# A two-layer graph kernel: VectorE's adjacency group is put directly behind x1, ahead of the statistics of x1

## The chip, the cores and the metric

One core of one Trainium2 chip runs the whole kernel. The metric is the device time of one launch in microseconds (us); the median of three runs of the kernel before is 2405.9 us.

## The reference

128 graphs of 128 nodes with 512 features, each with its own 128x128 weighted adjacency. Cut to what is computed:

```python
h = relu(layernorm(x));  A_hat = adj + I;  d = A_hat.sum(-1) ** -0.5
x1 = x + (A_hat * d[:, None] * d[None, :]) @ (h @ W + b)            # layer 0
xh = relu(layernorm(x1))                                           # layer 1
H = (adj != 0);  Be = 1 / H.sum(columns);  Dn = 1 / (H @ adj[0])
P = H @ diag(Be) @ H.T
h1 = layer_norm(relu(Dn * (P @ (xh @ W1.T)) + b1)) * gamma + beta   # 1024 wide
out = Dn * (P @ (h1 @ W2.T)) + b2 + xh + x1
```

## The kernel before

Every engine has its own instruction stream, written out by hand; semaphores tie them together, and each engine works strictly in its own order. One step of the software pipeline works on four graphs at once: `p = k+1` is prepared (statistics of x, adjacency, h0), `a = k` goes through layer 0, `c1 = k-1` through the first product of layer 1, `c2 = k-2` through the second, and `o = k-3` is written out. Steps -1 to 4 and the last ones are unrolled, those between run in a hardware loop, two steps to an iteration. There are 128 graphs, so 127 steps have both `a` and `p`.

Products are done in two parts, a high and a low one (names with `_hi`, `_lo`, `h`, `l`), three matmuls for each. What a step of TensorE does, in order: row sums and t0 (L times h0, 2 + 12 small matmuls, waits for `L_lo` and `h0_lo`); t1 (P times xh, 12 small ones, waits for `xh_lo`); t2 (P times hn, 24 small ones, waits for `hn_lo`); y1 (24 wide ones, line 331); y0 (12 wide ones); the transpose of the next graph's scaled adjacency (line 399, into `ps_at`, here AT); y2 (24 wide ones), with the incidence product P (lines 315, 316) after the first eight.

VectorE's order from the end of y0 to t2 is: `x1` (line 664, reads y0 out of PSUM), `bn_stats` of x1 (667), `inv_r` (671), `bn_aggr` (672), `hn` (677), `dn1` (682), `h0_lo` (689), `P_lo` (694), then the adjacency group: `ahat_T` (701, AT plus a diagonal), `H_T` with its count (703), `inv_b` (707), `L_hi` (712), `inv_t` (714), `L_lo` (716); behind it `xh_lo` (722) and `hn_lo` (728). All these write small or [128, 512] and [128, 1024] tiles in SBUF.

GpSimd in the same stretch first turns the statistics of h into `sc2` (lines 794 to 803), then waits for the statistics of x1 and turns them into `sc1` (807 to 813). Behind these come `sum2 = scr2 + b2` (818) and `base2 = sum2 + vq` (822), each 128x512, and then nothing until `base0` (762) of the next step. ScalarE makes `hn_hi` from sc2, `P_hi`, and from sc1 `xh` (518) and then `xh_hi` (522); `xh_lo` on VectorE needs both of these.

Of the kernel before, what the change touches and what calls it, by code (L numbers as in the profile page):

```python
# [5 lines left out]
def bass_adjacency_prenorm_two_layer_gnn_kernel(  # L6
# [38 lines left out]
    ALU = mybir.AluOpType  # L45
# [10 lines left out]
    P_SCALE = 2.0 ** 8  # L56
# [14 lines left out]
    with ctx:  # L71
        def sb(name, shape, dt=F32):
            return ctx.enter_context(nc.sbuf_tensor(name, shape, dt))

        def sem(name):
            return ctx.enter_context(nc.semaphore(name))
# [27 lines left out]
        diag_d = sb("diag_d", [128, N])  # L104
        adj_d = sb("adj_d", [128, N])
        ahat_T = sb("ahat_T", [128, N])
        L_hi, L_lo = sb("L_hi", [128, N], F16), sb("L_lo", [128, N], F16)
        H_T = sb("H_T", [128, 2, N], F16)
# [24 lines left out]
        rd0 = sb("rd0", [128, 2, 2])  # L133
# [5 lines left out]
        deg, cnt = sb("deg", [128, 2]), sb("cnt", [128, 2])  # L139
        inv_b, inv_t = sb("inv_b", [128, 1]), sb("inv_t", [128, 1])  # L140
# [17 lines left out]
        AT = ps_at[:, 0:N]  # L158
# [18 lines left out]
        s_diag, s_adjd, s_at, s_ht = sem("diag_D_ready"), sem("D_adj_ready"), sem("adjT_in_psum"), sem("HT_parts_ready")  # L177
        s_ahat, s_lth, s_lt = sem("ahatT_ready"), sem("LT_hi_ready"), sem("LT_lo_ready")
        s_stat0, s_ln0 = sem("stats0_ready"), sem("ln0_scalars_ready")
        s_h0, s_h0h, s_h0l = sem("h0_ready"), sem("h0_hi_ready"), sem("h0_lo_ready")  # L180
        s_t0, s_t0h, s_t0l = sem("t0_in_psum"), sem("t0_hi_ready"), sem("t0_lo_ready")
# [5 lines left out]
        s_p, s_ph, s_pl = sem("P_in_psum"), sem("P_hi_ready"), sem("P_lo_ready")  # L187
# [12 lines left out]
        s_cnt, s_cntsafe, s_cntinv, s_hbhi = sem("cnt_ready"), sem("cnt_safe"), sem("cnt_inverted"), sem("HB_hi_ready")  # L200
# [7 lines left out]
        def live(g, i):  # L208

            return not isinstance(i, int) or 0 <= g < NG  # L210
# [7 lines left out]
        def wait(eng, s, i, g):  # L218

            if not isinstance(i, int) or g >= 0:  # L220
                eng.wait_ge(s, i + (g + 1))
# [311 lines left out]
        def _(dve):  # L533
# [33 lines left out]
            def step(i, k):  # L567
                p, a, c1, c2, o = k + 1, k, k - 1, k - 2, k - 3
                if live(o, i):

                    m = o % 2
# [6 lines left out]
                                             in1=base2[:, m, :], op0=ALU.mult, op1=ALU.add).then_inc(s_out, 1)  # L578
                if live(c1, i):
# [4 lines left out]
                    m = c1 % 2  # L584
# [7 lines left out]
                                             in1=q[:, m:m + 1], op0=ALU.mult, op1=ALU.mult).then_inc(s_qdn, 1)  # L592
                if live(a, i):
# [8 lines left out]
                    m = a % 2  # L602
# [5 lines left out]
                                             in1=HB_hi[:, m, :], op0=ALU.mult, op1=ALU.subtract)\  # L608
# [8 lines left out]
                if live(p, i):  # L617

                    m = p % 2
# [4 lines left out]
                                             op0=ALU.not_equal, op1=ALU.mult, accum_out=deg[:, m:m + 1])\  # L624
# [9 lines left out]
                if live(c1, i):  # L634

                    m = c1 % 2
                    for c in range(NCH):
# [4 lines left out]
                                                 in1=b1_all[:, cols], op0=ALU.mult, op1=ALU.add)\  # L642
# [6 lines left out]
                if live(a, i):  # L649

                    m = a % 2
# [5 lines left out]
                if live(a, i):  # L657

                    m = a % 2
                    wait(dve, s_y0, i, a)  # L660
                    wait(dve, s_base0, i, a)
                    wait(dve, s_base2, i, a - 2)
                    wait(dve, s_xh, i, a - 2)
                    dve.scalar_tensor_tensor(out=x1[:, m, :], in0=ps_y0[:, :], scalar=1.0 / (L_SCALE * X_SCALE),  # L664
                                             in1=base0[:, :], op0=ALU.mult, op1=ALU.add).then_inc(s_x1, 1)
                    wait(dve, s_x1, i, a)
                    dve.bn_stats(raw1[:, :], x1[:, m, :]).then_inc(s_raw1, 1)  # L667
                    wait(dve, s_raw1, i, a)
                    wait(dve, s_ln1, i, a - 1)
                    wait(dve, s_degsafe, i, a)  # L670
                    dve.reciprocal(inv_r[:, :], inv_d[:, :]).then_inc(s_deginv, 1)
                    dve.bn_aggr(st1[:, :], raw1[:, :]).then_inc(s_stat1, 1)
# [6 lines left out]
                if live(a, i):  # L679
                    m = a % 2  # L680
                    wait(dve, s_deginv, i, a)
                    dve.scalar_tensor_tensor(out=dn1[:, m:m + 1], in0=deg[:, m:m + 1], scalar=0.0,
                                             in1=inv_r[:, :], op0=ALU.is_gt, op1=ALU.mult).then_inc(s_dn1, 1)
# [6 lines left out]
                if live(a, i):  # L690
                    m = a % 2
                    wait(dve, s_ph, i, a)
                    wait(dve, s_t2, i, a - 2)
                    dve.tensor_tensor(P_lo[:, m, :], PP, P_hi[:, m, :], ALU.subtract).then_inc(s_pl, 1)  # L694
                if live(p, i):

                    m = p % 2
                    wait(dve, s_at, i, p)
                    wait(dve, s_diag, i, p)
                    wait(dve, s_lt, i, p - 1)  # L700
                    dve.tensor_tensor(ahat_T[:, :], AT, diag_d[:, :], ALU.add).then_inc(s_ahat, 1)  # L701
                    wait(dve, s_p, i, p - 2)
                    dve.tensor_scalar(H_T[:, m, :], AT, 0.0, None, ALU.not_equal, ALU.add,  # L703
                                      accum_out=cnt[:, m:m + 1]).then_inc(s_cnt, 1)
                    wait(dve, s_cnt, i, p)

                    dve.tensor_scalar(inv_b[:, :], cnt[:, m:m + 1], 1.0, 1.0 / P_SCALE, ALU.max, ALU.mult)\
                       .then_inc(s_cntsafe, 1)
                    wait(dve, s_ahat, i, p)
                    wait(dve, s_ln0, i, p)  # L710
                    wait(dve, s_t0, i, p - 1)
                    dve.tensor_scalar(L_hi[:, :], ahat_T[:, :], rd0[:, m, 1:2], None, ALU.mult).then_inc(s_lth, 1)  # L712
                    wait(dve, s_cntsafe, i, p)
                    dve.reciprocal(inv_t[:, :], inv_b[:, :]).then_inc(s_cntinv, 1)
                    wait(dve, s_lth, i, p)
                    dve.scalar_tensor_tensor(out=L_lo[:, :], in0=ahat_T[:, :], scalar=rd0[:, m, 1:2],  # L716
                                             in1=L_hi[:, :], op0=ALU.mult, op1=ALU.subtract).then_inc(s_lt, 1)
                if live(a, i):
                    m = a % 2
                    wait(dve, s_xhh, i, a)  # L720
# [2 lines left out]
                                             op0=ALU.mult, op1=ALU.subtract).then_inc(s_xhl, 1)  # L723
# [7 lines left out]
                if first_graph(i, c1):  # L731
                    scale_v()
                    split_w2(range(KH - 2))

            every_step(ENG.DVE, step)


# [121 lines left out]
```

## Time and profile before

| what | value |
|---|---|
| runs, median (lowest, highest) | 2405.9 us (2403.88, 2405.99) |
| span of the profiled execution | 2403.2 us |
| time of that execution around its span | not given apart; the median of the runs lies 2.7 us above the span |
| TensorE matmul busy | 2211.9 us, 92% |
| VectorE busy | 2115.8 us, 88% |
| GpSimd busy | 1334.4 us, 56% |
| ScalarE busy | 1158.7 us, 48% |
| mean granted TensorE clock | 0.995 |
| one step inside the loop | 18.40 and 18.34 us in turn |

Busy is the time in which an engine had an instruction under way. An engine that waits inside an instruction, for a port for example, is counted as busy. Line numbers are those of the kernel before.

### The profile page before, as it was taken

Reading aid. Unit: us, or ns where it says so; the run is one execution under the profiler, and the core shown is the slowest. Engines: PE = TensorE matmul, PEld = TensorE weight load, DVE = VectorE, ACT = ScalarE, POOL = GpSimd, SP = SyncE. Lnnn points to the kernel's source line nnn. Section 1 sums busy time; section 2 is a strip of 40 time slices with the busy share of each in tenths; the row PEclk is TensorE's granted clock in tenths of the full one; section 3 lists DMA queues with packets and bytes.
Section 4 is the critical chain, followed back from the end, with each engine's and each line's share of the span. In section 5 each row is a group of like instructions: output and inputs, shape, how many; then the busy total and the mean of one; then the engine's idle time right before and its main releaser. Section 6 shows DMA issues by size and latency. Waiting matters only on the chain.

```text
span 2403.2 us, 48798 instructions
## 1 busy us (share of the span) xinstructions
PE 2211.9 (92%) x14480; PEld 1799.3 (75%) x14480; DVE 2115.8 (88%) x4754; ACT 1158.7 (48%) x1809; POOL 1334.4 (56%) x2574
## 2 busy tenths in 40 slices
PE   6999999999999999999999999999999999999998
PEld 4777777777777777777777777777777777777776
DVE  6889888988898898889888988988898889888986
ACT  4444445454444444444444444444444454544443
POOL 3555555555555555555555555555555555555553
PEclk8999999999999999999999999999999999999999
DMA  3111111011111111111111111111111111111110
GB/s 134 34 37 33 38 39 33 33 39 37 33 33 39 37 33 36 40 33 33 39 38 33 33 39 37 33 33 40 36 33 38 38 33 33 39 37 33 33 37 19
DMA packets 76558, 90.39 MB, mean 38 GB/s; under 512 B 8576, under 2 KB 41344, under 8 KB 76544
## 3 DMA queue, kind: packets, MB, share of 16 engines
q1 hardware_dynamic: 76544, 90.22, 12.5%
q8 instruction: 7, 0.11, 0.0%
q14 instruction: 7, 0.06, 0.0%
HBM read 56.63 MB, written 33.55 MB: 38 GB/s over the span
## 4 chain that ended last, share of the span: by engine, by line
PE 56%; DVE 33%; issue 8%; DVEq 1%; ACT 0%; DMA 0%; POOL 0%; SPq 0%; POOLq 0%; ACTq 0%
PE ps_y L331 29%; PE ps_t L331 15%; DVE L_hi L712 7%; PE ps_t L306 5%; DVE L_lo L716 4%; DVE raw L667 4%; DVE x L664 4%; PE ps_t L308 4%; PE ps_t L307 4%; DVE hn_lo L728 3%; DVE h_lo L689 2%; DVE xh_lo L722 2%; DVE P_lo L694 1%; DVE H_T L703 1%; DVE ahat_T L701 1%
## 5 line engine op out<-in xcount | busy, mean ns | idle before, releaser
L762 POOL TENSOR_TENSOR base<-scr,x_t 128x512 f32<-128x512 f32 x128 | 165.7, 1294 | 706.6 <-ACT scr L474 706.6
L450 ACT ACTIVATE h<-z 128x512 f32<-128x512 f32 x256 | 161.8, 632 | 453.6 <-DVE z L641 453.6
L565 DVE BATCH_NORM_STATS2 raw<-h 128x6 f32<-128x512 f32 x256 | 177.8, 695 | 189.2 <-ACT h L450 189.2
L331 PE MATMUL ps_y<-w1h,t1h 128*128 128x512 f32 x1024 | 288.7, 404 | 0.7 <-ACT t1h L459 0.7
L331 PE MATMUL ps_y<-w1h,t1l 128*128 128x512 f32 x1024 | 275.2, 391 | 2.1 <-DVE t1l L582 2.1
L331 PE MATMUL ps_y<-w1l,t1h 128*128 128x512 f32 x1024 | 276.5, 392 | 0.0
L331 PE MATMUL ps_t<-w2h,t2h 128*128 128x512 f32 x1024 | 268.8, 405 | 1.1 <-ACT t2h L467 1.1
L331 PE MATMUL ps_t<-w2l,t2h 128*128 128x512 f32 x1024 | 266.7, 402 | 0.0
L459 ACT ACTIVATE t1h<-ps_t 128x512 fp32r<-128x512 f32 x128 | 76.4, 597 | 379.0 <-PE ps_t L308 379.0
L331 PE MATMUL ps_t<-w2h,t2l 128*128 128x512 f32 x1024 | 253.4, 390 | 0.0
L505 ACT ACTIVATE hn_hi<-h,sc 128x1024 f16<-128x1024 f32 x128 | 159.0, 1242 | 143.5 <-POOL sc L803 143.5
L331 PEld LDWEIGHTS ps_y<-w1l,t1h 128*128 128x128 f32 x1024 | 193.4, 189 | 42.8
L331 PEld LDWEIGHTS ps_y<-w1h,t1l 128*128 128x128 f32 x1024 | 192.9, 188 | 43.4 <-DVE t1l L582 2.5
L331 PEld LDWEIGHTS ps_t<-w2h,t2l 128*128 128x128 f32 x1024 | 192.3, 188 | 41.2
L331 PEld LDWEIGHTS ps_t<-w2h,t2h 128*128 128x128 f32 x1024 | 183.8, 189 | 45.9 <-ACT t2h L467 1.4
L306 PE MATMUL ps_t<-P_hi,hn_hi 128*128 128x128 f16 x1024 | 180.0, 220 | 34.9 <-issue 17.6
L331 PEld LDWEIGHTS ps_y<-w1h,t1h 128*128 128x128 f32 x1024 | 184.1, 190 | 32.1 <-ACT t1h L459 1.0
L331 PEld LDWEIGHTS ps_t<-w2l,t2h 128*128 128x128 f32 x1024 | 183.4, 189 | 32.5
L641 DVE SCALAR_TENSOR_TENSOR z<-ps_y,dn,b_all 128x512 f32<-128x512 f32 x256 | 185.2, 723 | 2.1 <-PE ps_y L331 2.1
L308 PE MATMUL ps_t<-P_hi,hn_lo 128*128 128x128 f16 x1024 | 179.7, 220 | 0.0
L307 PE MATMUL ps_t<-P_lo,hn_hi 128*128 128x128 f16 x1024 | 179.7, 220 | 0.0
L716 DVE SCALAR_TENSOR_TENSOR L_lo<-ahat_T,rd,L_hi 128x128 f16<-128x128 f32 x128 | 178.0, 1390 | 0.0
(117 smaller groups left out, 5998.8 us busy)
## 6 DMA issues: line engine op xcount, KB each, us to landing
x_t<-in_x_dram SPq DMA_DIRECT2D x128, 256.0 KB, 2.6
out_dram<-out_t SPq DMA_DIRECT2D x128, 256.0 KB, 2.0
adj_t<-in_adj_dram SPq DMA_DIRECT2D x128, 64.0 KB, 2.0
wrow_t<-in_adj_dram SPq DMA_DIRECT2D x128, 64.0 KB, 3.0
stage<-in_W1T_dram SPq DMA_DIRECT2D x1, 2048.0 KB, 11.6
stage<-in_W2T_dram SPq DMA_DIRECT2D x1, 2048.0 KB, 8.8
stage<-in_W_dram SPq DMA_DIRECT2D x1, 1024.0 KB, 8.5
b_all<-in_b_dram SPq DMA_DIRECT2D x2, 256.0 KB, 8.1
```

Of the source, the lines that this page charges most:

```text
L306: pe.matmul(ps, lh, rh, start=True, stop=False)
L307: pe.matmul(ps, lh, rl, start=False, stop=False)
L308: return pe.matmul(ps, ll, rh, start=False, stop=True)
L331: mm = pe.matmul(ps, t[:, j * 128:(j + 1) * 128], w[:, j, cols], start=(n == 0 and j == 0), stop=(n == 2 and j == blocks - 1))
L450: act.activation(h[:, cols], z[:, cols], ACT.Relu).then_inc(s_h[c], 1)
L505: act.activation(hn_hi[:, :], h[:, :], ACT.Identity, bias=sc2[:, 1:2], scale=sc2[:, 0:1]).then_inc(s_hnh, 1)
L565: dve.bn_stats(raw2[:, c, :], h[:, c * CH:(c + 1) * CH]).then_inc(s_raw2, 1)
L641: dve.scalar_tensor_tensor(out=z[:, cols], in0=ps_y1[:, cols], scalar=dn1[:, m:m + 1], in1=b1_all[:, cols], op0=ALU.mult, op1=ALU.add)\
L664: dve.scalar_tensor_tensor(out=x1[:, m, :], in0=ps_y0[:, :], scalar=1.0 / (L_SCALE * X_SCALE), in1=base0[:, :], op0=ALU.mult, op1=ALU.add) ...
L712: dve.tensor_scalar(L_hi[:, :], ahat_T[:, :], rd0[:, m, 1:2], None, ALU.mult).then_inc(s_lth, 1)
L716: dve.scalar_tensor_tensor(out=L_lo[:, :], in0=ahat_T[:, :], scalar=rd0[:, m, 1:2], in1=L_hi[:, :], op0=ALU.mult, op1=ALU.subtract).then_i ...
L762: pool.tensor_tensor(base0[:, :], scr0[:, :], x_t[:, m, :], ALU.add).then_inc(s_base0, 1)
```

## The change

VectorE's adjacency group for graph p moves from behind `P_lo` to directly behind `x1`. The statistics of x1, `hn`, `dn1`, `h0_lo` and `P_lo` follow behind it in their old order. No instruction and no wait is added or taken away; in the steps without `p` the order is as before. The other engines' streams are the same.

```diff
                     dve.scalar_tensor_tensor(out=x1[:, m, :], in0=ps_y0[:, :], ...).then_inc(s_x1, 1)
-                    wait(dve, s_x1, i, a)
-                    dve.bn_stats(raw1[:, :], x1[:, m, :]).then_inc(s_raw1, 1)
...
-                    dve.tensor_tensor(P_lo[:, m, :], PP, P_hi[:, m, :], ALU.subtract).then_inc(s_pl, 1)
                 if live(p, i):
                     m = p % 2
                     wait(dve, s_at, i, p)
                     wait(dve, s_diag, i, p)
                     wait(dve, s_lt, i, p - 1)
                     dve.tensor_tensor(ahat_T[:, :], AT, diag_d[:, :], ALU.add).then_inc(s_ahat, 1)
...
                                              in1=L_hi[:, :], op0=ALU.mult, op1=ALU.subtract).then_inc(s_lt, 1)
+                if live(a, i):
+                    m = a % 2
+                    wait(dve, s_x1, i, a)
+                    dve.bn_stats(raw1[:, :], x1[:, m, :]).then_inc(s_raw1, 1)
+                    wait(dve, s_raw1, i, a)
+                    wait(dve, s_ln1, i, a - 1)
+                    wait(dve, s_degsafe, i, a)
+                    dve.reciprocal(inv_r[:, :], inv_d[:, :]).then_inc(s_deginv, 1)
+                    dve.bn_aggr(st1[:, :], raw1[:, :]).then_inc(s_stat1, 1)
...
+                    dve.tensor_tensor(P_lo[:, m, :], PP, P_hi[:, m, :], ALU.subtract).then_inc(s_pl, 1)
                 if live(a, i):
                     m = a % 2
                     wait(dve, s_xhh, i, a)
```

## Rows read from the trace of the kernel before

**Rows 1.** The page's first lines: span, busy time of each engine.

```profile
span 2403.2 us, 48798 instructions
PE 2211.9 (92%) x14480; PEld 1799.3 (75%) x14480; DVE 2115.8 (88%) x4754; ACT 1158.7 (48%) x1809; POOL 1334.4 (56%) x2574
```

**Rows 2.** Waits, whole span: who waited <- releaser: us, times, longest.

```profile
PE ps_at L353 <- DVE L_lo L716: 134.2, 127, 3.7
...
PE ps_t L306 <- DVE hn_lo L728: 17.3, 61, 0.3
```

**Rows 3.** Timeline, VectorE, an even step: start us, us, engine, line, operation.

```profile
1207.82 0.69 DVE L664 SCALAR_TENSOR_TENSOR x<-ps_t,base 128x512 f32<-128x512 f32 x1 [0.21 <-PE ps_t L331]
1208.54 0.69 DVE L667 BATCH_NORM_STATS2 raw<-x 128x6 f32<-128x512 f32 x1
...
1209.43 0.78 DVE L677 TENSOR_SCALAR hn<-h,sc 128x1024 f32<-128x1024 f32 x1
...
1210.20 0.68 DVE L689 TENSOR_TENSOR h_lo<-h,h_hi 128x512 f16<-128x512 f32 x1
1210.80 0.28 DVE L694 TENSOR_TENSOR P_lo<-ps_p,P_hi 128x128 f16<-128x128 f32 x1
...
1211.63 1.40 DVE L712 TENSOR_SCALAR L_hi<-ahat_T,rd 128x128 f16<-128x128 f32 x1
...
1213.06 1.38 DVE L716 SCALAR_TENSOR_TENSOR L_lo<-ahat_T,rd,L_hi 128x128 f16<-128x128 f32 x1
1214.37 0.68 DVE L722 SCALAR_TENSOR_TENSOR xh_lo<-xh,xh_hi 128x512 f16<-128x512 f32 x1
1214.97 1.21 DVE L728 TENSOR_TENSOR hn_lo<-hn,hn_hi 128x1024 f16<-128x1024 f32 x1
```

**Rows 4.** Timeline, VectorE, the odd step behind it: its x1 and hn_lo.

```profile
1226.22 0.69 DVE L664 SCALAR_TENSOR_TENSOR x<-ps_t,base 128x512 f32<-128x512 f32 x1
...
1233.45 1.21 DVE L728 TENSOR_TENSOR hn_lo<-hn,hn_hi 128x1024 f16<-128x1024 f32 x1
```

**Rows 5.** Timeline, GpSimd, the even step; in brackets the idle time before.

```profile
1209.59 0.67 POOL L807 TENSOR_TENSOR pw<-st,eps_one 128x1 f32<-128x1 f32 x1 [0.54 <-DVE st L672]
1210.22 0.71 POOL L808 TENSOR_TENSOR nm<-st,neg_one 128x1 f32<-128x1 f32 x1
...
1211.65 1.29 POOL L818 TENSOR_TENSOR sum<-scr,b_all 128x512 f32<-128x512 f32 x1
1213.02 1.27 POOL L822 TENSOR_TENSOR base<-sum,vq 128x512 f32<-128x512 f32 x1
```

**Rows 6.** Timeline, ScalarE, the even step.

```profile
1211.73 0.82 ACT L518 ACTIVATE xh<-x,sc 128x512 f32<-128x512 f32 x1 [1.15 <-POOL sc L813]
1212.58 0.63 ACT L522 ACTIVATE xh_hi<-xh 128x512 f16<-128x512 f32 x1
```

**Rows 7.** Timeline, VectorE, step 0, where GpSimd has no sum2 or base2.

```profile
27.14 0.28 DVE L701 TENSOR_TENSOR ahat_T<-ps_at,diag_d 128x128 f32<-128x128 f32 x1
...
27.77 0.29 DVE L712 TENSOR_SCALAR L_hi<-ahat_T,rd 128x128 f16<-128x128 f32 x1
...
28.09 0.35 DVE L716 SCALAR_TENSOR_TENSOR L_lo<-ahat_T,rd,L_hi 128x128 f16<-128x128 f32 x1
```

**Rows 8.** Timeline, three engines, step 127, which has no adjacency group.

```profile
2369.34 0.63 ACT L522 ACTIVATE xh_hi<-xh 128x512 f16<-128x512 f32 x1
...
2369.79 1.28 POOL L822 TENSOR_TENSOR base<-sum,vq 128x512 f32<-128x512 f32 x1
2370.01 1.61 DVE L722 SCALAR_TENSOR_TENSOR xh_lo<-xh,xh_hi 128x512 f16<-128x512 f32 x1
```

**Rows 9.** Timeline, TensorE: even step's row sums; the first product of the last t2.

```profile
1214.58 0.18 PE L353 MATMUL ps_at<-ones,L_hi 128*128 128x1 f16 x1 [1.01 <-DVE L_lo L716]
...
2388.93 0.22 PE L306 MATMUL ps_t<-P_hi,hn_hi 128*128 128x128 f16 x1 [2.53 <-issue]
```

**Rows 10.** Stretches: length, busy us (instructions) by engine, granted clock, DMA share, GB/s.

```profile
2371.00:2374.00 3.00, 0.91 (x14) 0.79 (x15) 3.00 (x3) 0.60 (x1) 1.57 (x2) 1.00 0.00 0
...
2389.00:2391.00 2.00, 2.00 (x24) 1.82 (x23) 0.49 (x1) 0.00 (x0) 0.00 (x0) 0.64 0.33 124
```

More of the change, by code:

```diff
@@ L665, in step @@
                                              in1=base0[:, :], op0=ALU.mult, op1=ALU.add).then_inc(s_x1, 1)
+                if live(p, i):
+                    m = p % 2
+                    wait(dve, s_at, i, p)
+                    wait(dve, s_diag, i, p)
+                    wait(dve, s_lt, i, p - 1)
+                    dve.tensor_tensor(ahat_T[:, :], AT, diag_d[:, :], ALU.add).then_inc(s_ahat, 1)
+                    wait(dve, s_p, i, p - 2)
+                    dve.tensor_scalar(H_T[:, m, :], AT, 0.0, None, ALU.not_equal, ALU.add,
+                                      accum_out=cnt[:, m:m + 1]).then_inc(s_cnt, 1)
+                    wait(dve, s_cnt, i, p)
+                    dve.tensor_scalar(inv_b[:, :], cnt[:, m:m + 1], 1.0, 1.0 / P_SCALE, ALU.max, ALU.mult)\
+                       .then_inc(s_cntsafe, 1)
+                    wait(dve, s_ahat, i, p)
+                    wait(dve, s_ln0, i, p)
+                    wait(dve, s_t0, i, p - 1)
+                    dve.tensor_scalar(L_hi[:, :], ahat_T[:, :], rd0[:, m, 1:2], None, ALU.mult).then_inc(s_lth, 1)
+                    wait(dve, s_cntsafe, i, p)
+                    dve.reciprocal(inv_t[:, :], inv_b[:, :]).then_inc(s_cntinv, 1)
+                    wait(dve, s_lth, i, p)
+                    dve.scalar_tensor_tensor(out=L_lo[:, :], in0=ahat_T[:, :], scalar=rd0[:, m, 1:2],
+                                             in1=L_hi[:, :], op0=ALU.mult, op1=ALU.subtract).then_inc(s_lt, 1)
+                if live(a, i):
+                    m = a % 2
                     wait(dve, s_x1, i, a)
@@ L694, in step @@
                     dve.tensor_tensor(P_lo[:, m, :], PP, P_hi[:, m, :], ALU.subtract).then_inc(s_pl, 1)
[L695 to L717, printed above, removed]
                 if live(a, i):
```

## The prediction

> **What bounds the kernel now.** I read the page's busy times first: TensorE works 92% of the span, VectorE 88% [rows 1], so either could be the bound, and only a step read instruction by instruction tells which part of it is whose. In the waits, TensorE's gaps are one kind: 134.2 us in 127 steps behind `L_lo`, 1.06 us a step, and a small one, 17.3 us, behind `hn_lo` [rows 2]. In the timeline I count from the start of x1. Even steps: x1 at 0 (1207.82), `L_lo` from 5.24 to 6.62, `xh_lo` 6.55, `hn_lo` 7.15 to 8.36 [rows 3]; y2 on TensorE ends at 5.75 (1214.58 less 1.01 of idle time) and t0 starts at 6.76 [rows 9]. The next x1 is at 18.40, and in the odd step `hn_lo` starts 7.23 behind x1 [rows 4]. From the end of `hn_lo` to the next x1 TensorE has t2, y1 and y0 without a gap, about 10 us that the change does not touch. So the time of a step is set by one number: when `hn_lo` starts, counted from x1. The wait that shows largest, for `L_lo`, is not the last one: even without it t2 would stand behind `hn_lo`.
>
> Two rows are strange: `L_hi` and `L_lo` take 1.40 and 1.38 us for 128 columns [rows 3], where in step 0 the same instructions take 0.29 and 0.35 [rows 7]. GpSimd's rows explain it. `sum2` runs from 1211.65 to 1212.94 and `L_hi`, begun at 1211.63, ends at 1213.03; `base2` runs from 1213.02 to 1214.29 and `L_lo` ends at 1214.44 [rows 3, 5]. In the other direction GpSimd's one-column lines 807 and 808 end at 1210.26 and 1210.93, each 0.05 behind the end of `hn` (1210.21) and `h0_lo` (1210.88) [rows 3, 5]. An instruction of one of these engines stands still until that of the other is done. So 2.14 us of VectorE's 8.4 are standing still (1.11 in `L_hi`, 1.03 in `L_lo`).
>
> **The change, part by part.** It moves six instructions with one accumulator read, issues no DMA, adds no wait, and passes no queue but VectorE's own.
>
> (1) The group's inputs. AT is transposed ahead of y2, before x1 ends, and y2 starts with it; `diag_d` is older. I cost the wait at nothing; the cover is x1's own 0.69 us.
>
> (2) The group's new length. An instruction of 512 columns lets the next one start after 0.60 (`h0_lo` to `P_lo` [rows 3]), so `ahat_T` starts at 0.61. From there to `L_lo` it is 0.95, and `L_lo` frees the engine 0.27 later (0.35 less 0.08 of overlap) [rows 7]. `L_hi` and `L_lo` fall at 1.24 to 1.91. GpSimd is idle there: line 807 starts at 1.77 after 0.54 us of idle time [rows 5], and it moves back with the statistics. So both take their step 0 length, and `bn_stats` starts at 1.83. Bounds: 0.1 less if the gaps for semaphores shrink; 0.2 more if an end of GpSimd's sc2 chain catches `L_hi`; and 2.14 more if both still stood still, the far end.
>
> (3) The statistics of x1 start at 1.83 in place of 0.72 [rows 3]: 1.11 later. What hangs on them moves by as much, since `hn` and `h0_lo` follow them as before and hold GpSimd's 807 and 808 as before. `xh` goes from 3.91 to 5.02 and `xh_hi` ends at 6.50 in place of 5.39 [rows 6]; `sum2` goes to 4.94; `base2` starts at 6.31 and ends at 7.58 (5.20 and 6.47 before [rows 5]).
>
> (4) VectorE behind it. `P_lo` ends at 4.37 (3.26 [rows 3] plus 1.11), and then VectorE idles, which it did not before, because `xh_lo` waits for `xh_hi` until about 6.53. What is queued behind the wait is `hn_lo`, and for that TensorE waits. The 2.14 us gained are spent here.
>
> (5) The collision. `base2` starts at 6.31, 0.2 before `xh_lo` can. So `xh_lo` meets the port taken, as `L_lo` did. The last step with x1 shows exactly this, since it has no adjacency group: `xh_hi` ends at 2369.97, `base2` has started at 2369.79 and ends at 2371.07, and `xh_lo`, begun at 2370.01, takes 1.61 and ends at 2371.62, 0.55 behind `base2` [rows 8]. In all the other loop steps it takes 0.68. So here it ends at 7.58 + 0.55 = 8.13, and `hn_lo` starts 0.08 earlier, at 8.05, and meets no GpSimd work, because the next `base0` needs work behind `hn_lo`.
>
> The Trainium skill says the same of the mechanism and against a softer reading: in "SBUF — State Buffer", section "Who interferes with whom", issue order decides who blocks, for the whole instruction, where a GpSimd instruction that reads SBUF meets a VectorE one with two SBUF inputs; a shared bandwidth is called a wrong intuition. If the two shared evenly, `xh_lo` would need about twice its 0.68 and end near 7.9, 0.2 earlier, and the sum below would be about 25 us less. The row of step 127 sides with the lock.
>
> (6) TensorE. t0 follows y2 at 5.75 without the 1.01 us gap; that gives nothing, since t1 now waits for `xh_lo` and t2 for `hn_lo`. t2 is later by what `hn_lo` is: 8.05 less 7.15 is 0.90 in even steps, 8.05 less 7.23 is 0.82 in odd ones, mean 0.86.
>
> **Sum.** Of the 127 steps with the group, steps 2 to 126 have this form: 125 x 0.86 = 107.5 us. Steps 0 and 1 have no `base2` in the way, but their `xh_lo` is 1.1 later each, with VectorE's weight splitting behind it: 2.2. So 2403.2 + 110 = 2513 of span, and with the 2.7 that the median lies above it 2515 us, 4.6% more.
>
> **The rivals.**
>
> Port order the other way: `xh_lo` gets in before `base2`. It would run at 6.53, `hn_lo` at 7.13: 0.02 and 0.10 earlier than now, about -7.5 us, with the first steps -5, so 2401, no change. For it: the margin is only 0.2 us. Against it: the margin is a difference of two fixed chains from the same sc1 (xh and `xh_hi`, 1.48 with their gap; `sum2` and its gap, 1.37), and step 127 shows it kept. Chance 0.07.
>
> Faster: the adjacency group was the bound and `xh_hi` is in time. Then VectorE is 2.14 shorter, `hn_lo` ends at 6.22, and TensorE is the bound: y2 until 5.75, t0 and t1 in about 1.4, t2 at 7.2 in place of 8.6; -1.4 x 125 gives 2230. It decides when `xh_lo` could start, unhindered, before 6.55; today's 134.2 us of waiting for `L_lo` speak for it [rows 2], the chain over GpSimd and ScalarE in (3) against. Chance 0.03.
>
> No clearing: `L_hi` and `L_lo` stay at 1.4. Then everything behind is 2.14 later still, 3.0 x 125: 2783. GpSimd's idle time speaks against. Chance 0.02.
>
> The clock. TensorE idles 1.3 us a step now and would idle 2.1. In 2371 to 2374 it worked 0.91 us of 3 and the granted clock stayed 1.00; after a gap of 2.53 us in the last t2 it fell to 0.64 [rows 9, 10], a mix of the 2.4 and the 1.2 GHz level. There 24 small matmuls took 2.00 us; at 0.91/14 each they take 1.56. If every t2 paid this, +0.44 x 125 on top: 2570. By the Trainium skill, "TensorE: Matmul & The Clock Gate", Part 1, the gate follows how busy the array has been recently; the rows say that gaps of this kernel's new size, between stretches of 10 us of full work, are too short. Chance 0.04.
>
> **How the numbers follow.** The forecast has 0.84: 2515, by its own bounds 2500 (0.1 less, 12 us, and the first steps free) to 2540 (0.2 more, 25 us). That is 2492 to 2542 with a little on both sides for the parts of a step that I took as unmoved; the rivals outside hold less than 2 in 10. A measurement of this kernel tells about 0.2% (5 us) from no change. Faster: the second rival and a part of the first, 0.05; within: the rest of the first, 0.05; slower: 0.90.
>
> **What would show it.** `L_hi` near 0.29 and `L_lo` near 0.35; `bn_stats` of x1 1.83 behind x1; a new wait of VectorE for `xh_hi`, about 2.2 us in each of 126 steps (some 270 us); `xh_lo` at 1.6; `hn_lo` 8.05 behind x1 in both kinds of step; TensorE's wait for `L_lo` gone, one of about 1.7 before t1 in its place; steps of 19.3 and 19.2 us. Wrong if `xh_lo` stays at 0.68 (the port order), or if VectorE does not wait for `xh_hi`.

## The result and the profile after

2584.97 us median (2581.31 to 2592.37, 4 runs) against 2404.89 us (2402.96 to 2405.99, 4 runs) before: a ratio of 1.0754, 95% interval 1.0733 to 1.0775. Slower, as forecast, but by 180 us where 110 were forecast. The profiled execution took 2588.4 us, 3.4 above that median, so the spans differ by a little more, 183.3 us. The page of the kernel after, its first lines and the row of `xh_lo`, now the costliest group of VectorE:

```profile
span 2586.5 us, 48798 instructions
...
PE 2279.3 (88%) x14480; PEld 1863.3 (72%) x14480; DVE 1962.5 (76%) x4754; ACT 1158.3 (45%) x1809; POOL 1332.0 (51%) x2574
...
L724 DVE SCALAR_TENSOR_TENSOR xh_lo<-xh,xh_hi 128x512 f16<-128x512 f32 x128 | 205.8, 1608 | 274.7 <-ACT xh_hi L522 274.7
```

VectorE's busy time fell by 153 us and TensorE's rose by 67, with the same number of instructions. Both are to be explained: the first is standing still that went away, the second is matmuls that took longer. VectorE in step 62, in the order of [rows 3]:

```profile
1256.28 0.69 DVE L664 SCALAR_TENSOR_TENSOR x<-ps_t,base 128x512 f32<-128x512 f32 x1 [0.21 <-PE ps_t L331]
1256.88 0.28 DVE L672 TENSOR_TENSOR ahat_T<-ps_at,diag_d 128x128 f32<-128x128 f32 x1
...
1257.52 0.29 DVE L683 TENSOR_SCALAR L_hi<-ahat_T,rd 128x128 f16<-128x128 f32 x1
...
1257.84 0.35 DVE L687 SCALAR_TENSOR_TENSOR L_lo<-ahat_T,rd,L_hi 128x128 f16<-128x128 f32 x1
1258.11 0.69 DVE L692 BATCH_NORM_STATS2 raw<-x 128x6 f32<-128x512 f32 x1
...
1262.80 1.58 DVE L724 SCALAR_TENSOR_TENSOR xh_lo<-xh,xh_hi 128x512 f16<-128x512 f32 x1 [2.16 <-ACT xh_hi L522]
1264.31 1.21 DVE L730 TENSOR_TENSOR hn_lo<-hn,hn_hi 128x1024 f16<-128x1024 f32 x1
```

ScalarE and GpSimd in the same step, against [rows 5, 6]:

```profile
1262.14 0.63 ACT L522 ACTIVATE xh_hi<-xh 128x512 f16<-128x512 f32 x1
```

```profile
1261.21 1.29 POOL L820 TENSOR_TENSOR sum<-scr,b_all 128x512 f32<-128x512 f32 x1
1262.58 1.26 POOL L824 TENSOR_TENSOR base<-sum,vq 128x512 f32<-128x512 f32 x1
```

Counted from x1 (1256.28), `L_hi` and `L_lo` have the short lengths of [rows 7], `bn_stats` starts at 1.83, VectorE waits 2.16 us for `xh_hi`, `base2` (6.30) is under way when `xh_lo` begins (6.52), and `hn_lo` starts at 8.03. `xh_lo` ends 0.54 behind `base2` (1264.38 and 1263.84), as in [rows 8].

What the forecast has not is on TensorE. Its row sums and t0 now follow y2 directly; then come two gaps, of 1.73 us ahead of t1 and 0.44 ahead of t2 (1.79 and 0.31 in odd steps). The first product of t1, of t2 and of y1 in this step (the last row is the first four of y1):

```profile
1264.49 0.22 PE L306 MATMUL ps_t<-P_hi,xh_hi 128*128 128x128 f16 x1 [1.73 <-issue]
...
1265.76 0.29 PE L306 MATMUL ps_t<-P_hi,hn_hi 128*128 128x128 f16 x1 [0.44 <-DVE hn_lo L730]
...
1268.26 1.50 PE L331 MATMUL ps_y<-w1h,t1h 128*128 128x512 f32 x4
```

Stretches of the kernel after (columns as in [rows 10]):

```profile
1262.00:1264.00 2.00, 0.76 (x15) 0.58 (x11) 1.20 (x1) 0.74 (x2) 1.76 (x2) 1.00 0.00 0
1264.00:1266.00 2.00, 1.07 (x15) 0.94 (x16) 2.00 (x3) 0.57 (x2) 0.00 (x0) 0.89 0.00 0
1266.00:1268.00 2.00, 2.00 (x22) 2.00 (x20) 1.97 (x8) 0.52 (x2) 0.00 (x0) 0.50 0.36 131
1268.00:1270.00 2.00, 2.00 (x11) 1.73 (x10) 0.52 (x2) 1.39 (x2) 0.00 (x0) 0.75 0.23 65
1270.00:1272.00 2.00, 2.00 (x10) 1.64 (x10) 2.00 (x5) 0.86 (x2) 1.30 (x1) 1.00 0.00 1
```

Two whole steps of it, step 64 and this one:

```profile
1296.30:1315.60 19.30, 17.13 (x115) 13.97 (x114) 15.17 (x38) 8.85 (x15) 10.28 (x21) 1.00 0.12 34
1256.30:1277.10 20.80, 18.63 (x115) 15.43 (x114) 15.27 (x38) 9.02 (x15) 10.47 (x22) 0.92 0.11 32
```

Behind the gaps the granted clock falls from the 2.4 to the 1.2 GHz level (0.50) and stays there for all of t2 and into y1, about 3 us, which costs about half of that. Step 64 kept its clock, with the same two gaps:

```profile
1304.51 0.22 PE L306 MATMUL ps_t<-P_hi,xh_hi 128*128 128x128 f16 x1 [1.73 <-issue]
...
1305.78 0.23 PE L306 MATMUL ps_t<-P_hi,hn_hi 128*128 128x128 f16 x1 [0.44 <-DVE hn_lo L730]
```

The two kinds are well apart. With the distances between the x1 of one step and the next, before and after, the 183.3 us between the two spans come out so:

| where | steps | us a step | us |
|---|---|---|---|
| full clock (19.23 and 19.29) | 82 | 0.884 | 72.5 |
| low clock (20.78 to 20.9), the same part | 42 | 0.884 | 37.1 |
| low clock, what comes on top | 42 | 1.54 | 64.7 |
| up to the third x1 (-0.83, +1.12, +1.01) | | | 1.3 |
| the last distance between two x1 | 1 | | 6.1 |
| behind the last x1 | | | 1.6 |

Of the 42, 36 are even steps and 6 odd ones. Step 2 stands in the first row, though it has the low clock too: it has it in the kernel before as well (19.45 us there, 20.46 here), so this is not the change's doing.

### The profile page after: what moved, and what is told of

The parts are those of the page before. It is cut to its first block, busy times and chain, and to the rows that moved or that the text cites. A ratio compares the mean times of both kernels' runs of the same rounds, so it can differ in the third digit from the quotient of the medians.

```text
span 2586.5 us, 48798 instructions
## 1 busy us (share of the span) xinstructions
PE 2279.3 (88%) x14480; PEld 1863.3 (72%) x14480; DVE 1962.5 (76%) x4754; ACT 1158.3 (45%) x1809; POOL 1332.0 (51%) x2574
## 4 chain that ended last, share of the span: by engine, by line
issue 25%; PE 24%; DVE 18%; POOL 16%; ACT 16%; DVEq 1%; DMA 0%; POOLq 0%; ACTq 0%; SPq 0%
PE ps_y L331 11%; DVE z L641 6%; ACT h L450 5%; PE ps_t L306 5%; ACT xh L518 4%; DVE raw L565 4%; PE ps_t L308 3%; PE ps_t L307 3%; POOL nm L810 3%; POOL pw L809 3%; ACT t2h L467 3%; ACT xh_hi L522 3%; DVE hn_lo L730 3%; POOL sc L803 3%; POOL sc L813 2%
## 5 line engine op out<-in xcount | busy, mean ns | idle before, releaser
L724 DVE SCALAR_TENSOR_TENSOR xh_lo<-xh,xh_hi 128x512 f16<-128x512 f32 x128 | 205.8, 1608 | 274.7 <-ACT xh_hi L522 274.7
L331 PE MATMUL ps_y<-w1h,t1h 128*128 128x512 f32 x1024 | 308.8, 426 | 0.7 <-ACT t1h L459 0.7
L306 PE MATMUL ps_t<-P_hi,xh_hi 128*128 128x128 f16 x512 | 92.9, 219 | 227.8 <-issue 226.2
L306 PE MATMUL ps_t<-P_hi,hn_hi 128*128 128x128 f16 x1024 | 222.3, 248 | 50.8 <-DVE hn_lo L730 26.8
L518 ACT ACTIVATE xh<-x,sc 128x512 f32<-128x512 f32 x128 | 104.4, 815 | 286.8 <-POOL sc L815 286.8
L331 PEld LDWEIGHTS ps_y<-w1h,t1h 128*128 128x128 f32 x1024 | 200.8, 208 | 34.9 <-ACT t1h L459 1.0
L306 PEld LDWEIGHTS ps_t<-P_hi,xh_hi 128*128 128x128 f16 x512 | 49.9, 97 | 243.0 <-issue 241.2
L308 PE MATMUL ps_t<-P_hi,hn_lo 128*128 128x128 f16 x1024 | 224.4, 249 | 0.0
L307 PE MATMUL ps_t<-P_lo,hn_hi 128*128 128x128 f16 x1024 | 223.8, 249 | 0.0
```

The source lines that it names most:

```text
L306: pe.matmul(ps, lh, rh, start=True, stop=False)
L307: pe.matmul(ps, lh, rl, start=False, stop=False)
L308: return pe.matmul(ps, ll, rh, start=False, stop=True)
L331: mm = pe.matmul(ps, t[:, j * 128:(j + 1) * 128], w[:, j, cols], start=(n == 0 and j == 0), stop=(n == 2 and j == blocks - 1))
L518: act.activation(xh[:, m, :], x1[:, m, :], ACT.Relu, bias=sc1[:, 1:2], scale=sc1[:, 0:1]).then_inc(s_xh, 1)
L724: dve.scalar_tensor_tensor(out=xh_lo[:, :], in0=xh[:, m, :], scalar=X_SCALE, in1=xh_hi[:, :], op0=ALU.mult, op1=ALU.subtract).then_inc(s_x ...
```

## The experiments

Theory A, from here on: the statistics of x1, 1.11 us later, let `xh_lo` come due while `base2` has the port (0.88 us a step), and TensorE's longer gaps cost clock (1.54 us in a third of the steps). Rival B: the long steps are slow for another reason, and the clock is a companion. Rival C: the later statistics alone set the time, the port only shows on top. Rival D: nothing but the place of the group matters, the port never does.

**Is it the clock?** Two kernels fill the first gap with work that has no other effect: t0's twelve products are issued three times (e1) or twice (e5).

```diff
-                    for j in range(KI):
+                    for j in [*range(KI)] * 3:
                         f = slice(j * 128, (j + 1) * 128)
                         mm = thin(ps_t0[:, f], (h0_hi[:, f], h0_lo[:, f]), (L_hi[:, :], L_lo[:, :]))
```

> The changed kernel with TensorE's twelve t0 products issued three times over (the same result, two of the three without use), which fills 1.3 us of its 1.73 us gap in front of t1. Theory A: the 42 long steps of the changed kernel (20.8 in place of 19.25 us) are those in which the granted clock fell to 1.2 GHz behind two gaps of TensorE, and have no other cause. Then they vanish: all steps 19.2 to 19.3, hn_lo still 8.05 to 8.11 behind x1, about 2515 to 2520 us. Rival: something else of these steps is slow (a transfer, ScalarE's t2h) and the clock only goes with it: long steps stay, about 2585 us. Rival 2: more work on TensorE costs time by itself: over 2600.

> The changed kernel with TensorE's t0 products issued twice, so that its gap in front of t1 is about 1.06 us in place of 1.73 (0.4 with three times). The kernel before had gaps of 1.01 and 0.28 us a step and kept its clock. Theory A: a gap of 1.06 and one of 0.4 are about what the clock bore before; no or few long steps, 2515 to 2530 us. Rival: any idle time beyond that of before (1.3 us a step, here 1.5) costs clock in proportion: half of the 67 us that the full gap cost, about 2550 us.

Measured: 2518.11 us (2517.3 to 2518.94), ratio 1.0469 (1.0452 to 1.0487), and 2517.73 us, 1.0467 (1.0450 to 1.0485). Of the 42 long steps counted above none is left in e1 or e5. Over 20 us is only step 2 in e5 (20.59), the step that has the low clock in the kernel before too. `xh_lo` still takes 1.61 us and the usual steps are 19.22 and 19.29. The gaps ahead of t1 and t2, in e1:

```profile
1273.72 0.22 PE L306 MATMUL ps_t<-P_hi,xh_hi 128*128 128x128 f16 x1 [0.38 <-issue]
...
1274.99 0.23 PE L306 MATMUL ps_t<-P_hi,hn_hi 128*128 128x128 f16 x1 [0.44 <-DVE hn_lo L730]
```

and in e5:

```profile
1273.46 0.22 PE L306 MATMUL ps_t<-P_hi,xh_hi 128*128 128x128 f16 x1 [1.05 <-issue]
...
1274.73 0.23 PE L306 MATMUL ps_t<-P_hi,hn_hi 128*128 128x128 f16 x1 [0.44 <-DVE hn_lo L730]
```

TensorE got 24 matmuls more a step and the kernel became 67 us faster. That settles rival B: what was changed is only how long TensorE idles, and the long steps went with it. It is not in proportion either: with 1.05 and 0.44 us the cost is gone, with 1.73 and 0.44 it is 67 us. Some 5 of these 67 us are not in the long steps but in the last distance between two x1 (24.4 us in the kernel after, 19.1 in e1 and e5; see the open points). e7, further down, adds a case: there TensorE's one gap a step is 1.4 to 1.5 us, more than any of the kernel before inside the loop (1.03), and from step 3 on no step has the low clock:

```profile
1220.53 0.22 PE L306 MATMUL ps_t<-P_hi,xh_hi 128*128 128x128 f16 x1 [1.49 <-ACT xh_hi L522]
```

**Is it the port?** One wait ahead of GpSimd's `base2` moves it behind `hn_lo`, in the kernel after (e2) and in the kernel before (e3); in e4, the kernel before, `sum2` has it too.

```diff
                     wait(pool, s_psum2b, i, c1)
+                    wait(pool, s_hnl, i, c1)
```

> The changed kernel with one wait more: GpSimd's base2 waits until hn_lo is done, so that it can't meet xh_lo. Theory A: xh_lo is held by base2 for 0.95 us; without it xh_lo takes 0.68 from 6.53, hn_lo starts at 7.13, steps are 18.3 as before the change, TensorE's gaps are under 1 us and the clock stays: about 2400 us, the change costs nothing. Rival: the later statistics alone (1.11 us) set the time, the port only shows on top; then steps of 19.2 stay and the time is above 2500 us. Rival 2: base2 in its new place holds up something else (HB_lo, base0): between 2400 and 2500.

Measured: 2400.03 us (2397.97 to 2400.5), ratio 0.9977 (0.9968 to 0.9987). `xh_lo` and `hn_lo` in e2, x1 being at 1206.46:

```profile
1212.99 0.69 DVE L724 SCALAR_TENSOR_TENSOR xh_lo<-xh,xh_hi 128x512 f16<-128x512 f32 x1 [2.16 <-ACT xh_hi L522]
1213.60 1.22 DVE L730 TENSOR_TENSOR hn_lo<-hn,hn_hi 128x1024 f16<-128x1024 f32 x1
```

The statistics are as late as before and VectorE waits the same 2.16 us, and the kernel costs nothing more than the one before the change. Rival C falls. TensorE's first gap is 0.82 us, and the clock came back with it: one edit on GpSimd took back 185 us.

> The kernel before with the same wait (base2 behind hn_lo). Theory A: L_lo falls from 1.38 to 0.35, xh_lo starts at about 5.5, hn_lo at 6.1, steps of about 17.3: about 2275 us, faster than both kernels. Rival: the port is only where the wait shows, something else (TensorE) bounds the step: 2395 to 2405 us.

> The kernel before with sum2 and base2 both behind hn_lo. Theory A: L_hi falls to 0.29 too, but xh_lo then waits for xh_hi until 5.42, so hn_lo starts at 6.03: only 0.1 us a step better than with base2 alone, about 2265 us. Rival: each held instruction counts in full, 1.1 us a step more: about 2140 us.

Measured: e3 2266.72 us, ratio 0.9425 (0.9410 to 0.9441); e4 2255.68 us, 0.9379 (0.9363 to 0.9395). `L_hi`, `L_lo`, `xh_lo` in e3, with x1 at 1209.99:

```profile
1213.81 1.39 DVE L712 TENSOR_SCALAR L_hi<-ahat_T,rd 128x128 f16<-128x128 f32 x1
1215.23 0.35 DVE L716 SCALAR_TENSOR_TENSOR L_lo<-ahat_T,rd,L_hi 128x128 f16<-128x128 f32 x1
1215.50 0.68 DVE L722 SCALAR_TENSOR_TENSOR xh_lo<-xh,xh_hi 128x512 f16<-128x512 f32 x1
```

and in e4, with x1 at 1204.82:

```profile
1208.76 0.29 DVE L712 TENSOR_SCALAR L_hi<-ahat_T,rd 128x128 f16<-128x128 f32 x1
1209.08 0.35 DVE L716 SCALAR_TENSOR_TENSOR L_lo<-ahat_T,rd,L_hi 128x128 f16<-128x128 f32 x1
1210.25 0.69 DVE L722 SCALAR_TENSOR_TENSOR xh_lo<-xh,xh_hi 128x512 f16<-128x512 f32 x1 [0.82 <-ACT xh_hi L522]
```

So in the kernel before, the hold in `L_lo` was worth 139 us. The hold in `L_hi`, as long, is worth 11 more, because VectorE then waits for `xh_hi`. Both times are 8 or 9 us under what was expected. An equal stall in the same chain is worth what is late next.

**What the place of the group costs by itself.** With `sum2` and `base2` behind both `hn_lo` and `xh_lo`, and `hn_lo` made ahead of `xh_lo`, neither the port nor `hn_lo` is in the way: e6 on the kernel before, e7 on the kernel after.

```diff
+                    wait(pool, s_hnl, i, c1)
+                    if live(a, i):
+                        wait(pool, s_xhl, i, a)
                     wait(pool, s_psum2a, i, c1)
...
-                if live(a, i):
-                    ... xh_lo
                 if live(c1, i):
                     ... hn_lo
+                if live(a, i):
+                    ... xh_lo
```

> The kernel before, sum2 and base2 behind both hn_lo and xh_lo, and VectorE makes hn_lo ahead of xh_lo. Nothing of VectorE is then in TensorE's way: hn_lo at 4.4, xh_lo at 5.54, t0, t1 and t2 follow y2 without a gap, steps of 17.0 us, about 2226 us. Rival: the order of these two is without effect, since t2 needs both: 2255 us as with both late.

> The changed kernel with the same edits. No collision is left, hn_lo is done early (5.5), and what sets t2 is the chain of the later statistics alone: xh_lo at 6.53, done at 7.21, t1 at 7.3, t2 at about 8.05, steps of 17.85 us, about 2345 us. So the group ahead of the statistics costs 0.85 us a step here where nothing hides it. Rival: the later statistics were only ever a cost through the port: then as the kernel before with these edits, 2226 us.

Measured: e6 2225.27 us, ratio 0.9252 (0.9236 to 0.9267), steps of 16.94 and 17.03. e7 2407.24 us, 1.0008 (0.9999 to 1.0018): 62 us more than expected. VectorE's `hn_lo` in e7 and GpSimd's last two instructions for sc1 (lines 811 and 813 of before):

```profile
1216.93 1.22 DVE L724 TENSOR_TENSOR hn_lo<-hn,hn_hi 128x1024 f16<-128x1024 f32 x1
```

```profile
1216.82 0.54 POOL L813 TENSOR_TENSOR sc<-pw,neg_half 128x1 f32<-128x1 f32 x1
1217.44 0.76 POOL L815 TENSOR_TENSOR sc<-nm,sc 128x1 f32<-128x1 f32 x1
```

The one-column product took 0.76 us in place of 0.19 and ended 0.05 behind `hn_lo`: I had moved a long VectorE instruction onto the chain that everything now waited for. e9 is e7 with `hn_lo` waiting for sc1 as well.

```diff
                     wait(dve, s_t2, i, c1 - 1)
+                    if live(a, i):
+                        wait(dve, s_ln1, i, a)
                     dve.tensor_tensor(hn_lo[:, :], hn[:, :], hn_hi[:, :], ALU.subtract).then_inc(s_hnl, 1)
```

> The changed kernel with sum2 and base2 late and hn_lo ahead of xh_lo as in the run before last but one, and with hn_lo also waiting until sc1 is done. The run without this wait gave 2407 in place of 2345: hn_lo, at 4.28, held GpSimd's last instruction for sc1 (0.76 in place of 0.19 us). If that was all, xh is back at 5.02, xh_lo at 6.53, steps 17.85, about 2345 us. Rival: something else in the new order costs the 0.56 us; then still about 2407 us.

Measured: 2341.64 us (2336.82 to 2343.97), ratio 0.9728 (0.9712 to 0.9745), steps of 17.81 and 17.90, `xh_lo` at 6.53. Against e6 the place of the group costs 0.87 us a step, with neither `xh_lo` nor `hn_lo` held in either. The 124 steps make 108 of the 116 us; another 5.7 are in the last distance between two x1 (22.9 against 17.2 us). So the change has a price of its own, which the kernel before hid behind `hn_lo` and the port.

**The group behind the statistics.** In e8 and e10 the group stands directly behind `bn_aggr`, ahead of `hn`; e8 has `sum2` and `base2` behind `hn_lo`, e10 is the move alone.

```diff
                     dve.reciprocal(inv_r[:, :], inv_d[:, :]).then_inc(s_deginv, 1)
                     dve.bn_aggr(st1[:, :], raw1[:, :]).then_inc(s_stat1, 1)
+                if live(p, i):
+                    ... the group, ahat_T to L_lo
                 if live(c1, i):
                     ... hn
```

> The adjacency group one place further back than the change puts it: behind bn_aggr, with hn, dn1, h0_lo, P_lo behind it, and sum2 and base2 behind hn_lo. The statistics keep their time (bn_stats at 0.72), and GpSimd's 807 to 813 run beside the group and are no more held by hn and h0_lo, so xh_hi is done near 4.5 in place of 5.39; L_hi and L_lo may be held by single GpSimd instructions (up to 0.5 us). xh_lo at 4.6, hn_lo at 5.2 to 6.4: TensorE without a gap, steps of 17.0 us, about 2226 us. Rival: hn and h0_lo 1.3 us later shift hn_lo as much, or the held L_hi gives back the gain: 2255 us or more.

> The adjacency group behind bn_aggr alone, sum2 and base2 where they were. hn at 2.82 then stands where sum2 wants to start (2.95), and hn, h_lo, xh_lo and hn_lo on one side and sum2 and base2 on the other take turns at the port. Theory A: sum2 gets in between hn and h_lo or behind h_lo, base2 between xh_lo and hn_lo or ahead of both; hn_lo starts between 6.0 and 7.4: 2260 to 2430 us, clearly above the 2214 with sum2 and base2 late. Rival: the place of the group alone decides and the port costs nothing here: about 2214 us.

Measured: e8 2213.86 us (2210.68 to 2219.23), ratio 0.9206 (0.9189 to 0.9223), the fastest of all; e10 2405.43 us, 0.9998 (0.9989 to 1.0008). e8 is 12 us under what was expected: 14 of its 124 steps took 16.2 to 16.3 us in place of 16.9 or 17.0, and why is not shown. In e10 the port holds other instructions. VectorE, x1 being at 1205.44:

```profile
1208.25 1.94 DVE L702 TENSOR_SCALAR hn<-h,sc 128x1024 f32<-128x1024 f32 x1
1210.12 1.24 DVE L707 SCALAR_TENSOR_TENSOR dn<-deg,inv_r 128x1 f32<-128x1 f32 x1
1211.28 0.68 DVE L714 TENSOR_TENSOR h_lo<-h,h_hi 128x512 f16<-128x512 f32 x1
...
1212.68 1.21 DVE L730 TENSOR_TENSOR hn_lo<-hn,hn_hi 128x1024 f16<-128x1024 f32 x1
```

and GpSimd:

```profile
1208.34 1.31 POOL L820 TENSOR_TENSOR sum<-scr,b_all 128x512 f32<-128x512 f32 x1
1209.72 1.61 POOL L824 TENSOR_TENSOR base<-sum,vq 128x512 f32<-128x512 f32 x1
```

`hn` loses 1.16 us and `dn1`, one column, 1.09: together the 2.14 that `L_hi` and `L_lo` lost before, give or take 0.1, and `hn_lo` starts 7.24 behind x1, where it did in the odd steps of [rows 4]. This is the picture of 88 of the steps 2 to 126. In the other 37 `hn` takes 0.81 us, and `dn1` (1.27) and `xh_lo` (1.56) are held. My guess of which instructions take turns was wrong (I had neither `hn` nor `dn1` held), the time was within the range. Rival D falls: with the group in one and the same place e8 and e10 are 192 us apart.

## Why the prediction was wrong, and where it was right

The direction and the forecast's own six terms held, step by step, and e1 shows it, where the clock is taken out: 2518 against the 2515 forecast. What failed is a seventh term, TensorE's clock, that the sum put at nothing.

(1), (2) The inputs were there: `ahat_T` at 0.60, `L_hi` 0.29, `L_lo` 0.35, `bn_stats` at 1.83. Right to 0.02 us.

(3), (4) `xh_hi` ended at 6.49 (6.50 forecast); VectorE waited for it for 274.7 us (270).

(5) `base2` first, then `xh_lo`, in all steps of this form; `hn_lo` at 8.03 and, in the steps of the other parity, at 8.11, where I had 8.05 for both. I had read `base2` in an even step only; in odd ones it starts 0.08 us later (6.38 against 6.30 behind x1), as it did before (5.29 against 5.20). So the loss is nearly the same in both kinds, 0.89 and 0.88, and not 0.90 and 0.82. The Trainium skill's rule ("SBUF — State Buffer", section "Who interferes with whom") fits the holds shown here of instructions with two SBUF inputs (`L_lo`, `xh_lo`, `dn1`), and in both directions: e7 shows it with VectorE as the holder. `L_hi` and `hn`, with one tensor as input, were held just as well (1.40 us in [rows 3], 1.94 in e10).

(6) and the sum: 110 us forecast; 72.5 + 37.1 + 1.3 = 110.9 measured. The idle time of TensorE was right too, 1.73 us ahead of t1.

The step that failed is the rival called the clock, to which I gave 0.04 and a price of 0.44 us a step. Its condition was there in the forecast itself: I had worked out that TensorE would idle 2.1 us a step. I took the stretch of 2371 to 2374 in [rows 10] as proof that such gaps are harmless. In length it was a fair match, 0.98 and 1.38 us:

```profile
2371.72 0.22 PE L306 MATMUL ps_t<-P_hi,xh_hi 128*128 128x128 f16 x1 [0.98 <-issue]
...
2373.92 0.22 PE L306 MATMUL ps_t<-P_hi,hn_hi 128*128 128x128 f16 x1 [1.38 <-issue]
```

But it is one case, and one case of something that comes in a third of the steps proves little; in the kernel after, 81 steps show the same as that row, and 42 the opposite. The price was off as well: I charged t2's 24 products by a stretch of mixed clock (0.64). The clock was at the 1.2 GHz level throughout t2 and for the start of y1, and it cost 1.54 us where it came, 0.52 us a step on the mean of the 124: near my 0.44 by accident. With that rival at its measured price (65 us) the sum would have been 2580; at mine it was 2570. The rest, about 5 us, lies at the end of the loop.

By the Trainium skill, "TensorE: Matmul & The Clock Gate", Part 1, the gate follows the array's recent activity. The trace agrees, and the case adds the numbers. Step 2 apart, gaps of 1.73 and 0.44 us lost the clock in 36 of 61 even steps, and gaps of 1.79 and 0.31 in 6 of 62 odd ones. With 1.05 and 0.44 us (e5) and with one gap of 1.4 to 1.5 (e7) no step lost it.

The range's upper end, 2542, left this out. It held everything that I took as one of my own terms, and none of what a longer idle time triggers in the chip.

Open: why the same gaps lose the clock in one step and not in the next (most long ones are every fourth step: 10, 14, 18, 22, 26 and so on); and 5 us at the end of the loop. There TensorE's t1 starts late, 11.85 us behind x1 in place of 8.21:

```profile
2534.30 0.26 PE L306 MATMUL ps_t<-P_hi,xh_hi 128*128 128x128 f16 x1 [5.36 <-issue]
```

`xh_lo` had ended at 2530.56, so 3.7 us of the 5.36 are not a wait that the profile shows. The granted clock is at the low level behind it as well (0.66 on the mean of 2531 to 2541), which fits the rest of the 5 us. The place is where TensorE's stream leaves the hardware loop. The last distance between two x1 is 24.4 us here, 23.6 in e2, 22.9 in e9, 23.0 in e10 and 20.6 in e8, each 3.6 to 5.3 us more than a usual step of that kernel, but 18.3 before and 19.1 in e1 and e5. No run here isolates the cause.

## What to carry to other kernels

Time an in-order engine's instructions by what they have to do; where the same shape takes three or four times as long in one place, find the neighbour that ends just before it, and ask of every reordering which instruction will stand there next. Moving the victim only picks another one (e10: no gain); moving the neighbour that nobody waits for took 139 us (e3) and, with the group behind the statistics, 191 us (e8).

Work put ahead of the head of a chain through three engines is paid once nothing else is late, however short it has become: of the 1.11 us by which the statistics came later, 0.87 a step (e9 against e6).

When a forecast makes TensorE idle longer in one piece, give the clock loss a real chance and not a corner, and price it for the work that follows the gap. One stretch in the trace before where the clock stayed does not rule it out; nor does a longer gap make it certain (e7).

## What the runs showed of the hardware that I had not expected

A one-column VectorE instruction with two SBUF inputs is held as long as a wide one: `dn1` 1.24 us in e10, against 0.15 in the kernel after. Surplus work can pay: 24 surplus small matmuls a step made the kernel 67 us faster (e1), and 12 did as much (e5). Between steps 3 and 125 no single gap was longer than 1.8 us, and the clock still fell. And TensorE's clock cost was invisible in the page's row of tenths, which shows 9 in 39 of its 40 slices after as before; only the mean (0.966 against 0.995) and the narrow stretches show it.
